# Two attention layers in one kernel: the first lead's transposes in PSUM banks of their own, the first attention's projections one slot later, and a new order for the slots without projections, the norms and the second lead

## What is computed

```python
x = x + _L0_attn_ref(_layernorm(x), L0_attn_w_qkv, L0_attn_w_dense)      # causal, 32 heads of 128, 8 groups
x = x + _L0_ffn_ref(_layernorm(x), L0_ffn_A, L0_ffn_B, L0_ffn_Wr)        # 64 rank-16 experts, top 16 gates
x = x + _L1_attn_ref(_layernorm(x), Wq, Wk, Wv, Wo, q_norm_w, k_norm_w)  # RMS norm of q and k, ALiBi bias
x = x + _L1_ffn_ref(_layernorm(x), ...)                                  # NF4 weights, silu(g) * u
```

## Time and profile before

| | |
|---|---|
| median of 3 runs | 1890.41 us (1886.05 to 1893.25) |
| the profiled execution | 1885.1 us, span 1883.4 us |
| PE busy | 1770.8 us, 94% of the span |
| DVE, ACT, POOL busy | 1317.8, 880.5, 776.8 us |
| TensorE clock, mean over the span | 0.968 of full |

### The profile page before, as it was taken

One profiled execution on the slowest core, in us unless ns is written; L12 is line 12 of the kernel. 1 busy time (PEld: TensorE's weight loads), 2 busy tenths in 40 slices (PEclk: granted clock), 3 DMA queues, 4 the chain that ended last, 5 costly groups with the idle time before them and its releaser, 6 DMA issues.

```text
span 1883.4 us, 28746 instructions
## 1 busy us (share of the span) xinstructions
PE 1770.8 (94%) x8856; PEld 1464.6 (78%) x8856; DVE 1317.8 (70%) x2316; ACT 880.5 (47%) x2289; POOL 776.8 (41%) x924
## 2 busy tenths in 40 slices
PE   7999999999999889987899999999999996889999
PEld 6887888888888768875678787878787885668887
DVE  4678878788887855424678777777777776755555
ACT  2565565565566443221444444444444443544543
POOL 4334435344353441224545363535454523244442
PEclk9999999999999988888899999999999998999999
DMA  3121222122121201000101010000001002022111
GB/s 117 52 84 45 78 78 72 56 84 78 50 88 63 98 1 57 1 1 29 33 12 45 24 31 28 28 28 28 28 28 28 23 0 67 12 57 77 56 56 45
DMA packets 47711, 87.77 MB, mean 47 GB/s; under 512 B 6576, under 2 KB 6576, under 8 KB 47536
## 3 DMA queue, kind: packets, MB, share of 16 engines
q1 hardware_dynamic: 47664, 87.19, 15.0%
HBM read 77.73 MB, written 9.44 MB: 46 GB/s over the span
## 4 chain that ended last, share of the span: by engine, by line
PE 71%; DVE 11%; issue 6%; ACT 5%; POOL 4%; DMA 1%; POOLq 0%; DVEq 0%; SPq 0%; ACTq 0%
PE ring L300 13%; PE ring L301 13%; PE ring L302 13%; PE scores L300 4%; PE scores L301 4%; PE scores L302 4%; PE turned L300 3%; PE turned L301 3%; PE turned L302 3%; PE scores L645 3%; PE turned L731 2%; DVE lv_early L546 2%; ACT p L751 2%; PE turned L724 1%; PE turned L695 1%
## 5 line engine op out<-in xcount | busy, mean ns | idle before, releaser
L300 PE MATMUL ring<-xt_hi,w_lo 128*128 128x512 f32 x768 | 307.7, 401 | 6.3 <-DVE k_raw L858 3.4
L301 PE MATMUL ring<-xt_lo,w_hi 128*128 128x512 f32 x768 | 306.4, 399 | 0.0
L302 PE MATMUL ring<-xt_hi,w_hi 128*128 128x512 f32 x768 | 306.0, 398 | 0.0
L742 ACT CAST pt_hi<-turned 128x512 fp32r<-128x512 f32 x192 | 100.8, 592 | 263.2 <-PE turned L724 262.2
L300 PE MATMUL ring<-wd_hi,ot_lo 128*128 128x512 f32 x512 | 209.1, 408 | 11.8 <-DVE ot_lo L842 7.3
L302 PE MATMUL ring<-wd_hi,ot_hi 128*128 128x512 f32 x512 | 203.3, 397 | 0.0
L301 PE MATMUL ring<-wd_lo,ot_hi 128*128 128x512 f32 x512 | 203.3, 397 | 0.0
L563 POOL TENSOR_SCALAR sq_hi<-sq 128x512 fp32r<-128x512 f32 x80 | 55.4, 693 | 301.0 <-ACT sq L768 301.0
L300 PEld LDWEIGHTS ring<-xt_hi,w_lo 128*128 128x128 f32 x768 | 146.9, 191 | 40.1 <-DVE k_raw L858 3.8
L302 PEld LDWEIGHTS ring<-xt_hi,w_hi 128*128 128x128 f32 x768 | 146.5, 191 | 35.3
L301 PEld LDWEIGHTS ring<-xt_lo,w_hi 128*128 128x128 f32 x768 | 146.8, 191 | 32.0
(11 more groups left out here) (228 smaller groups left out, 4468.4 us busy)
## 6 DMA issues: line engine op xcount, KB each, us to landing
w_raw<-w_attn_dram SPq DMA_DIRECT2D x96, 256.0 KB, 3.2
wd_raw<-w_dense_dram SPq DMA_DIRECT2D x64, 256.0 KB, 2.7
code_early<-codes_dram SPq DMA_DIRECT2D x28, 256.0 KB, 2.9
absmax_early<-absmax_dram SPq DMA_DIRECT2D x56, 128.0 KB, 3.2
kept_dram<-deq_early SPq DMA_DIRECT2D x28, 256.0 KB, 2.0
stage<-kept_dram SPq DMA_DIRECT2D x28, 256.0 KB, 2.7
code_late<-codes_dram SPq DMA_DIRECT2D x14, 256.0 KB, 2.8
absmax_late<-absmax_dram SPq DMA_DIRECT2D x28, 128.0 KB, 2.9
```

What stands on the lines that cost most here:

```text
L300: nc.tensor.matmul(o, l_lo, r_hi, start=start, stop=False)
L301: nc.tensor.matmul(o, l_hi, r_lo, start=False, stop=False)
L302: return nc.tensor.matmul(o, l_hi, r_hi, start=False, stop=stop)
L742: nc.scalar.copy(pt_hi[:, j, :, :], turned[:, j, :, :]).then_inc(s_pt_hi, 1)
```

## The change

It has five parts.

1. The first lead. `lead_turn` gives each of the eight token tiles' transposes a bank of its own or one long free (`lead_bank`: the banks of the scores and of `turned`), where before all went through the two ring banks. DVE writes tiles 0, 1, 2, 4 and 5, ACT 3, 6 and 7; four 128x128 matmuls (`warm`) follow the first four transposes. POOL's first weight split waits for DVE's third write.
2. The first attention's tiles stand one slot later: K, Q0, Q1 of the second half in slot 0 and Q2, Q3, V in slot 1, those of the next group's first half in slots 2 and 3. The lead computes three tiles fewer (6 for 9), and the last group's slot 1 has three tiles and a `v_turn` that it had not.
3. The slots without tiles (`last_slot_steps`) put `pv` ahead of the softmax, the next batch's scores behind `out` 1, a norm's statistics between `max` and `normalise`, and the transposes of a written norm into the next slot ahead of its `pv`.
4. In the experts stage `gated` of batch 3 comes ahead of `out` of batch 2; odd batches get a buffer of their own for it.
5. The second lead: the K tile comes ahead of the norm's root, POOL's split of the output weights stands behind the fifth square (`split_wd`), V of the second half is computed in the lead, and Q1 of the second half at the head of the first slot. The second attention's four slots of a turn are as before.

```diff
@@ -95,62 +95,64 @@
-def slot_steps(b, rms, projects, first=False):
...
+def slot_steps(b, rms):
+    if rms:
+        half, ahead = (0 if b in (1, 2) else 1), (0 if b == 0 else 1)
+        tiles = [K, Q0, Q1] if b in (1, 3) else [Q2, Q3, V]
+    else:
+        half, ahead = (1, 0) if b in (0, 1) else (0, 1)
+        tiles = [K, Q0, Q1] if b in (0, 2) else [Q2, Q3, V]
     t = [("tile", x, half, ahead) for x in tiles]
...
+    roots = rms and b in (1, 3)
+    s = [("pt_split",)] + ([] if rms else [("dq_lines", 0)])
+    s += [("scores", 0), ("mask", 0), ("max", 0, 0)] + t[0:1] + [("max", 1, 0), ("exp", 0), ("normalise", 0)] + t[1:2]
+    s += [] if rms else [("exp", 1)]
+    s += [("q_rms_turn", 1 if b == 1 else 0)] if roots else []
+    s += [("pv",)] + ([("exp", 1)] if rms else [])
+    s += [("roots", 1 if b == 1 else 0)] if roots else []
+    s += [("k_rms", half)] if rms and tiles[0] == K else []
+    s += t[2:3] + [("normalise", 1)] + ([] if rms else [("dq_lines", 1), ("dq_top", 0)]) + [("out", 0)]
+    s += [("v_turn", half)] if tiles[-1] == V else []
+    s += [("k_norm", 1 if b == 1 else 0)] if roots else []
+    s += [] if rms else [("dq_top", 1)]
+    if rms:
+        s += [("out", 1), ("q_rms", half, 0 if tiles[0] == K else 1)]
+    else:
+        s += [("dq_value",), ("out", 1)]
+    return s + [("transpose",)]
+def first_slot_steps(rms):
+    softmax = [[("scores", 0), ("mask", 0), ("max", 0, 0)], [("max", 1, 0), ("exp", 0), ("normalise", 0)], [("exp", 1)]]
+    if rms:
+        s = [("tile", Q1, 1, 0)] + softmax[0] + [("q_rms", 1, 0), ("tile", Q2, 1, 0)] + softmax[1]
+        s += [("tile", Q3, 1, 0)] + softmax[2] + [("normalise", 1), ("w_next", V), ("q_rms", 1, 1)]
+        return s + [("transpose",)]
+    s = softmax[0] + [("tile", K, 1, 0)] + softmax[1] + [("tile", Q0, 1, 0)] + softmax[2] + [("tile", Q1, 1, 0)]
+    return s + [("normalise", 1), ("dq_first",), ("transpose",)]
+def last_slot_steps(b, rms):
+    if b == 1 and not rms:
+        return [step for step in slot_steps(1, rms) if step[0][0:3] != "dq_"][:-1] + [("scores", 1), ("transpose",)]
+    s = [("pt_split",)] + ([("norm_turn", 0)] if b == 3 else []) + ([("scores", 0)] if b == 1 else [])
+    if rms and b == 1:
+        s += [("q_rms_turn", 1), ("roots", 1), ("pv",), ("k_norm", 1), ("mask", 0)]
+    else:
+        s += [("mask", 0), ("pv",)]
+    s += [("max", 0, 0), ("exp", 0), ("max", 1, 0)]
+    s += norm_begin([b - 2], "pool") if b >= 2 else []
+    s += [("normalise", 0), ("exp", 1), ("normalise", 1), ("out", 0)]
+    if rms and b in (1, 2):
         s += [("ffn_hi", k) for k in (2 * b - 2, 2 * b - 1)] + [("ffn_lo", k) for k in (2 * b - 2, 2 * b - 1)]
...
+    s += [("norm_write", b - 2, "act")] if b >= 2 else []
+    s += [("out", 1)] + ([("scores", 1)] if b < 3 else [])
     return s + [("transpose",)]
@@ -165,25 +167,26 @@
...
-        return norm_begin([3], "dve") + [
-            ("tile", K, 0, 0), ("tile", V, 0, 0), ("tile", Q0, 0, 0), ("norm_turn", 3), ("k_rms", 0),
-            ("tile", Q1, 0, 0), ("v_turn", 0), ("q_rms", 0, 0), ("tile", Q2, 0, 0), ("tile", Q3, 0, 0), ("q_rms", 0, 1),
-            ("tile", K, 1, 0), ("q_rms_turn", 0), ("roots", 0), ("tile", Q0, 1, 0), ("k_norm", 0), ("k_rms", 1),
-            ("tile", Q1, 1, 0), ("q_rms", 1, 0)]
+        s = [("norm_stats", [3]), ("tile", K, 0, 0), ("norm_root", [3], "dve"), ("norm_write", 3, "dve")]
+        s += [("tile", Q0, 0, 0), ("tile", V, 0, 0), ("k_rms", 0), ("tile", Q1, 0, 0), ("v_turn", 0), ("norm_turn", 3)]
+        s += [("q_rms", 0, 0), ("tile", Q2, 0, 0), ("tile", Q3, 0, 0), ("tile", V, 1, 0), ("q_rms", 0, 1)]
+        s += [("split_wd",), ("tile", K, 1, 0), ("v_turn", 1), ("q_rms_turn", 0), ("roots", 0), ("tile", Q0, 1, 0)]
+        return s + [("k_rms", 1), ("k_norm", 0)]
...
-    s += [("norm_write", 0, "dve"), ("norm_write", 2, "dve"), ("norm_write", 1, "act"), ("norm_turn", 0)]
-    s += [("norm_turn", 1), ("norm_write", 3, "act"), ("tile", K, 0, 0), ("norm_turn", 2), ("tile", Q0, 0, 0)]
-    s += [("norm_turn", 3)] + [("tile", x, 0, 0) for x in (Q1, Q2, Q3, V)] + [("v_turn", 0)]
-    return s + [("tile", x, 1, 0) for x in (K, Q0, Q1)]
+    s += [("lead_write", "dve", [0, 1, 2]), ("lead_write", "act", [3]), ("lead_turn", [0, 1, 2, 3])]
+    s += [("lead_write", "dve", [4, 5]), ("lead_write", "act", [6, 7]), ("warm",), ("tile", K, 0, 0)]
+    s += [("lead_turn", [4, 5]), ("tile", Q0, 0, 0), ("lead_turn", [6, 7])]
+    return s + [("tile", x, 0, 0) for x in (Q1, Q2, Q3, V)] + [("v_turn", 0)]
 def tail_steps():
-    return [("pt_split",)] + norm_begin([2], "pool") + [("pv",), ("norm_write", 2, "act"), ("out", 0), ("out", 1),
-                                                        ("norm_turn", 2)]
+    return [("pt_split",), ("norm_turn", 1), ("pv",)] + norm_begin([2], "pool") + [("norm_write", 2, "act"), ("out", 0), ("out", 1),
+                                                                 ("norm_turn", 2)]
...
+LEAD_STEPS = ("lead_write", "lead_turn", "warm")
...
+            def lead_bank(t):
+                own = [scores1[:, 0:2, :], scores1[:, 2:4, :], scores0, turned[:, 0, :, :], turned[:, 1, :, :],
+                       turned[:, 2, :, :], turned[:, 0, :, :], turned[:, 1, :, :]][t]
+            def pe_lead(pe, step):
+                    for t in step[1]:
+                        written, count = lead_written[t]
+                        pe.wait_ge(written, count)
+                        if t >= 6:
+                            pe.wait_ge(s_lead_lo, t - 2)
+                        for c in range(DC):
+                            at = slice(c * P, (c + 1) * P)
+                            ins = nc.tensor.transpose(lead_bank(t)[:, at], lv[:, t, at], ident[:, :])
+                        ins.then_inc(s_lead_turn, 1)
+                elif step[0] == "warm":
+                    for k in range(4):
+                        nc.tensor.matmul(ring[:, 0, k * P:(k + 1) * P], ident[:, :], ident[:, :], start=True, stop=True)
...
+                        if X == K and not rms and (b is None or (isinstance(g, int) and g == 0 and b == 0)):
+                            pe.wait_ge(s_lead_lo, 4 * half + 4)
...
+                    elif step[0] == "w_next":
+                        pool.wait_ge(s_ring_full, pool_ring.value())
+                        pool_split_w(pool, step[1])
+                    elif step[0] == "split_wd":
+                        pool_split_wd(pool)
...
-            s += [("norm_write", 1, "act"), ("out", 2), ("norm_turn", 1)] + gated(3) + norm_begin([2], "pool")
+            s += gated(3) + [("norm_write", 1, "act"), ("out", 2), ("norm_turn", 1)] + norm_begin([2], "pool")
...
-            gated_hi, gated_lo = (w[:, :, :].rearrange("p h d -> p (h d)").rearrange("p (c q) -> p c q", q=SEQ)
...
+            gated = [tuple(w[:, :, :].rearrange("p h d -> p (h d)").rearrange("p (c q) -> p c q", q=SEQ)
+                           for w in (wd_hi, wd_lo))]
+            gated.append(tuple(sb(f"gated_{name}", [P, EC, SEQ], F32R, scope) for name in ("hi", "lo")))
...
+                        if b == 1 and step[2] == 0:
+                            eng.wait_ge(s_split, 2 * UNITS + 1)
```

151 lines of the change are left out of this document (68 added, 83 removed).

## The result

The changed kernel takes **1867.38 us** (median of 5 runs, 1865.52 to 1871.51) against 1890.41 (median of 5, 1884.34 to 1893.25). The ratio is 0.9899, 95% interval 0.988 to 0.9918: about 1.0% faster, or 19 us. The two medians alone are 23.0 apart, which is more than this interval allows; in the three later sets of runs the kernel before had medians of 1885.8 to 1887.6. The forecast was 1865.0, in a range of 1849 to 1880.

What follows compares the result with a forecast made beforehand. TensorE, busy 94% of the span, bounds the kernel, leaving its idle time and low clock; gains of 5.0, 1.3, 1.0, 4.7, 10.9 and 2.5 sum to 25.4, so 1885.1 becomes 1859.7, plus 5.3 gives 1865.0 us, range 1849 to 1880.

Steps and rivals of the forecast that it cites:

- Part 1: First lead and first slot: earlier K tile 2.8, ring waits 2.5, clock 0.8, less 1.1 for bare waits; gain 5.0 us.
- The clock term: Half-clock loss: 0.8 us taken back in the first lead; 5.3 falling to 3.6 in the first attention's last slots.
- The step that named the banks as the cause: First lead: two later ring-bank waits of 1.24 us go, as those transposes have banks of their own; 2.5 us.
- Part 2: First attention's seven turns: 2.7 us gained by earlier output weights, 1.4 lost by later dequantised lines; gain 1.3.
- a sign of being wrong: First attention's turns: a new wait of over 1 us in slot 2 would show the forecast wrong.
- the fourth rival: Slower: first attention's slot 1 becomes POOL-bound; gain gone at 3.6 us a turn, over 0.5% slower from 5.0; chance 0.06.
- The other term: First attention's slot 1: output weights come about 0.44 us earlier at out 0, 2.7 over six turns.
- Part 3, first attention: Last slots: clock loss falls 1.7 us, idle rises 0.7 as xn's write stands ahead of pt_hi; gain 1.0.
- The rule that spoke against part 3: Last slots: DVE instructions with two SBUF inputs block GpSimd's SBUF reads, so all four chains meet normalise, about 1 us each.
- Part 4: Experts: the 3.54 us wait for wd_lo goes, clock gives 1.7, gates' bare waits cost 0.5; gain 4.7.
- Part 5: Second lead and first slot: 3.40 us wait for k_raw goes, POOL's queue leaves 7.0 idle; 78.5 falls to 67.6, gain 10.9.
- Second attention's last slots: The 5.54 us wait ahead of pv is taken apart; idle 21.4 to 20.3, clock loss 8.4 to 7; gain 2.5.

Runs made afterwards that it cites:

- experiment 3: The changed kernel without its part 2: first attention's tiles in the slots of before, nine tiles in the first lead; 1873.14 us.
- experiment 6: The changed kernel with the first lead's eight transposes through two banks in turn, those of scores1; 1871.78 us (one run).
- experiment 1: The changed kernel with SP's loads of the next group's Q2, Q3 and V weights issued at the end of slot 0 in the first attention; 1865.74 us.
- experiment 2: The changed kernel with GpSimd's three weight splits in slot 1 of the first attention's turns behind dq_value and the centring of the next codes; 1859.47 us.
- experiment 5: The changed kernel with part 3 undone in both attentions, the first attention's slot 1 keeping its tiles; 1871.75 us (one run).
- experiment 4: The changed kernel with ScalarE's write of xn moved behind the next slot's pt_split and TensorE's transposes of xn behind pv; 1857.14 us.
- experiment 8: The changed kernel without its part 4: gated of batch 3 behind out of batch 2 again, buffers kept; 1870.92 us (one run).

## Why the prediction was right, and where it wasn't

The total was right: 1867.38 for 1865.0. It was right by some luck. The 25.4 were worked out against the profiled execution of before, and against it the spans are only 17.7 shorter; 7.7 are missing, as much as the seven turns missed. That the medians lie 23.0 apart comes from this set of runs of before, 3 to 5 us above its three later ones. And inside the sum terms of both signs cancel. Point by point:

- **Part 1** (5.0, measured 5.6). The K tile started at 18.58, not 17.7, but the first write of that execution also stood 1.0 later, at 14.13 for the 13.14 of the earlier trace rows; from the first write on it is 4.45 for 7.39, a gain of 2.9 for the 2.8 forecast. The two waits of 1.24 went. The clock term was too small for this execution: 0.8 taken, and the half-clock stretch of the earlier trace rows went wholly, up to 2.7. The normalise that stands bare in the first slot cost 2.86 of waiting, where I had 1.1; against experiment 3, which has no such wait and nine tiles, the K tile to the slot's end is 7.6 shorter for 9.0 of work (35.30 for 42.91), so the price is 1.4. In seven of the nine profiles with this lead and first slot a stretch of 3.4 or 6.8 us at half clock begins near the end of that wait (at 51.0 to 52.7), and then the next slot takes 20.7 to 22.1 for 20.11; the changed kernel's profile happens to have none. The step that named the banks as the cause was wrong in size: against two banks they give 0.8 (experiment 6).
- **Part 2** (gain of 1.3, measured loss of 6.5) is where the sum failed. The step is "ACT's dequantised lines of slot 2 come up to 1.7 later. ... most of that is slack; I charge 0.2 for each of seven turns". They came 3.0 later (5.6 for 2.6) in the turn shown, since the weight load waited too (2.11) and the splits and `dq_top` held each other up, and slot 2 lost 1.6 a turn (21.27 on average for its bare 19.66). The wait of 1.19 there (to 1.47 in other turns) is over the 1 us that the prediction gave as a sign of being wrong. The mechanism of the fourth rival was the right one, at a third of the price from which it decides. Experiments 1 and 2 show the chain: without the load's wait 3.9 of slot 2's 9.7 come back, with the splits behind `dq_value` all of them. The other term held: slot 1 takes 21.1 as before although it now has a `v_turn` of 0.45, so 0.4 a turn was gained there, forecast 0.44.
- **Part 3, first attention** (1.0, measured 1.2) is right only in the sum. The tiles in slot 1 gained 5.6 and the new order lost 4.4 (experiment 5). The reason that I gave for the loss, the write of `xn` ahead of `pt_hi`, is what experiment 4 shows, at 7.0. The clock term failed: by the prediction's own reckoning (busy x (1-c)) it was to fall from 5.3 to 3.6, and the row gives 60.08 x 0.11 = 6.6, at 0.89 for the 0.90 of before. What I missed is that the slot needs the tiles as cover for the output weights (8.25, experiment 3).
- **The rule that spoke against part 3.** All four chains met the normalise: 5.71, 5.72, 5.49 and 5.49 for 16 instructions, where two that met only the normalise's smaller part took 4.64 in the second attention before, and the tails', which met none, took 4.35. VectorE's instruction, begun first, kept its length (1.22 at 659.21), and GpSimd's, begun 0.01 later, took 1.26 for 0.2. The rule holds here. Its price in the second attention is 0.85 a chain; in the first both were at 5.62 and 5.64 already.
- **Part 4** (4.7, measured 5.3). The 3.54 went as forecast, but putting it back costs only 2.2 (experiment 8). The 1.7 for the clock is more like 3.
- **Part 5** (10.9, measured 9.9). GpSimd's queue showed where it was forecast, though not at one place: TensorE waits 1.03 for `sq_lo` of K at 879.17, 4.43 at 884.30 behind VectorE's `xn` ahead of the roots, and 4.47 for `sq_lo` in the first slot, 9.9 together, for the 7.0 of the queue and 3.5 of the first slot that I gave. The sum came out nearer than its terms: by the window row idle time is 16.4 for my 13.6 and the clock's part 6.3 for my 5.1, while busy time less that part is 46.1 where I let 48.9 stand.
- **Second attention's last slots** (2.5, measured 4.8; by experiment 5 the order is worth 6.5). The wait of 5.54 went, and the waits for `xn` in its place were 1.16, 2.65 and 2.66. Idle time is 19.2 for my walk's 20.3, and the clock's part 53.34 x 0.09 = 4.8 for my 7.
- **Not forecast:** the last layer's 2.0. TensorE waits longer for its first dequantised weights, 2.99 for the 1.90 of before, and there are 10.2 us at half clock in that stage for 6.8. But this isn't shown to be the change's: the stage took 248.2 to 251.4 in the kernels here, all of which share it, and the one of experiment 6 has a wait of 1.90, 6.8 us at half clock and 248.18. And the second attention's turns took 631.1 to 635.1 in the kernels here, which all share them, longest where 7.7 us or more of them were at half clock: no difference of single executions under 4 us should be read from that stretch.

The last layer's two rows, before and after:

```profile
1667.22 0.47 PE L300 MATMUL ring<-w_hi,h_lo 128*128 128x512 f32 x1 [1.90 <-POOL w_lo L1396]
```

```profile
1647.95 0.47 PE L307 MATMUL ring<-w_hi,h_lo 128*128 128x512 f32 x1 [2.99 <-POOL w_lo L1468]
```

## What to carry to other kernels

A helper engine that is busy 41% of the time can still set the pace where its queue is in order: what counts is which instruction stands ahead of the one that the next slot needs. Ask for each moved step what is now behind it on every queue, and put work that nobody waits for soon (here the weight splits) behind work that somebody does. A cover that a reordering takes away may be hiding an engine that isn't in the picture: with the new order and no tiles in the slot, GpSimd's splits of the output weights came out as a wait of 8.25. And one reordering can have opposite signs in two places: the new order of the last slots was worth 6.5 in one attention and cost 4.4 in the other.

## What the runs showed of the hardware

VectorE's instructions with two SBUF inputs and GpSimd's instructions on SBUF made each other wait where they met in the rows read: the one that had begun first kept its length, and the other ended up to about its own length behind it (experiment 1). The larger `dq_top` took up to 2.31 for 1.22, `w_lo` up to 2.14 for 1.3, one small instruction of the chain 1.26 for 0.2. Starting GpSimd's splits 2.1 us earlier (experiment 1) therefore brought `dq_value` forward by 0.34 only in the turn shown.

How much of a stretch runs at half clock differs from one kernel's profile to the next where the order is the same: 23.5 to 36.6 us in the experts stage, with the changed order, and 0 to 7.9 us in the seven turns of the second attention, which took 631.1 to 635.1.
